# Context attention with 16 heads: GpSimd's softmax product of a unit as one operation or as two, first tile ahead

## The reference

```python
q = (query @ Wq + bq).reshape(B, Nq, H, D).transpose(0, 2, 1, 3)
k = (key_value @ Wk + bk).reshape(B, Nkv, H, D).transpose(0, 2, 1, 3)
v = (key_value @ Wv + bv).reshape(B, Nkv, H, D).transpose(0, 2, 1, 3)
attn = jnp.einsum('bhqd,bhkd->bhqk', q, k) * scale
attn = jnp.clip(attn, -CLAMP, CLAMP)
attn = jax.nn.softmax(attn, axis=-1)
x = jnp.einsum('bhqk,bhkd->bqhd', attn, v).reshape(B, Nq, Cq)
return x @ Wo + bo
```

## Time and profile before

| | |
|---|---|
| median of 3 runs | 3066.73 us |
| the profiled execution | 3068.3 us |
| its span on the core | 3066.6 us |
| mean granted clock of PE, of full speed | 0.92 |
| PE busy (matmul) | 2623.7 us, 86% |
| PE's weight loads busy | 1882.0 us, 61% |
| DVE busy | 1443.6 us, 47% |
| ACT busy | 1294.5 us, 42% |
| POOL busy | 891.2 us, 29% |
| POOL, L1438, all three context attentions | 436.0 us, 192 operations |

### The profile page before, as it was taken

How to read it: one execution, slowest core, us unless ns; L and a number is a source line. 1 busy time by engine, 2 the same in 40 slices (tenths; PEclk the granted TensorE clock), 3 DMA queues, 4 the chain that set the end, 5 groups by cost and what they waited for, 6 DMA issues and landing times. The chain is left out here.

```text
span 3066.6 us, 55571 instructions
## 1 busy us (share of the span) xinstructions
PE 2623.7 (86%) x18272; PEld 1882.0 (61%) x18273; DVE 1443.6 (47%) x3490; ACT 1294.5 (42%) x3858; POOL 891.2 (29%) x572
## 2 busy tenths in 40 slices
PE   5746999979787989999599877899959997988899
PEld 2335666656455556666489734566649996876554
DVE  5695888931534234444522376666650003553200
ACT  1334677832443123333233222677733332772222
POOL 3264455510001022222133243455522222330000
PEclk8867999979898999999799987999979998998999
DMA  2000000000241010000367600000045554004100
GB/s 105 1 0 28 17 20 20 16 30 0 58 105 52 0 45 21 15 15 15 126 207 237 204 33 33 22 15 20 15 181 171 177 184 134 1 17 113 56 12 13
DMA packets 108488, 194.38 MB, mean 63 GB/s; under 512 B 56532, under 2 KB 81060, under 8 KB 96596
## 3 DMA queue, kind: packets, MB, share of 16 engines
q1 hardware_dynamic: 93986, 166.80, 16.9%
q0 software_dynamic: 6816, 18.62, 2.1%
q10 hardware_dynamic: 7570, 7.47, 0.8%
HBM read 174.16 MB, written 18.71 MB: 63 GB/s over the span
## 5 line engine op out<-in xcount | busy, mean ns | idle before, releaser
L1438 POOL TENSOR_TENSOR L_xattn_p<-L_xattn_p,L_xattn_ri 112x1500 f32<-112x1500 f32 (+1 forms) x192 | 436.0, 2271 | 566.2 <-DVE L_xattn_ri L1746 566.2
L1651 ACT ACTIVATE L_xattn_pT<-ps 125x448 f32<-125x448 f32 (+1 forms) x576 | 256.5, 479 | 358.4 <-PE ps L1542 357.8
L1542 PEld LDWEIGHTS ps<-ident,L_xattn_p 112*125 112x125 f32 x1920 | 255.8, 191 | 121.2 <-ACT L_xattn_pT L1651 41.7
L1542 PE MATMUL ps<-ident,L_xattn_p 112*125 112x112 f32 x1920 | 292.0, 284 | 41.8 <-POOL L_xattn_p L1438 29.1
L1663 ACT ACTIVATE L_xattn_p<-L_xattn_sa,L_xattn_ng 112x375 f32<-112x375 f32 x512 | 304.8, 601 | 16.4 <-DVE L_xattn_ng L1762 10.7
L1093 PEld LDWEIGHTS ps<-L_ffn_xsT,L_ffn_w 128*128 128x128 f32 x2240 | 265.4, 195 | 7.0 <-issue 1.9
L1093 PE MATMUL ps<-L_ffn_xsT,L_ffn_w 128*128 128x128 f32 x2240 | 266.5, 278 | 2.4 <-ACT L_ffn_xsT L1123 2.4
L276 POOL TENSOR_TENSOR ln_rstd<-ln_tmp,half 112x8 f32<-112x8 f32 x26 | 44.4, 1722 | 703.7 <-DVE ln_tmp L225 526.5
L1155 DVE TENSOR_TENSOR L_ffn_y<-ps,L_ffn_pack 128x256 f32<-128x256 f32 x70 | 29.7, 425 | 365.4 <-PE ps L1102 365.4
L1102 PE MATMUL ps<-L_ffn_weights,L_ffn_hT 128*128 x840 | 192.9, 379 | 2.3 <-DVE L_ffn_hT L1167 2.3
L1564 PE MATMUL ps<-L_xattn_kT,L_xattn_qm 32*112 32x375 f32 (+1 forms) x1280 | 173.3, 524 | 11.2 <-DVE L_xattn_ng L1759 5.8
(11 more groups left out here) (415 smaller groups left out, 5113.2 us busy)
## 6 DMA issues: line engine op xcount, KB each, us to landing
L_ffn_w<-in_L_ffn_experts SPq DMA_DIRECT2D x74, 1024.0 KB
L_xattn_src<-in_ctx SPq DMA_DIRECT2D x48, 375.0 KB, 3.0
L_attn_toeplitz<-L_attn_h SPq DMA_DIRECT2D x4, 3136.0 KB, 24.0
L_ffn_weights<-in_L_ffn_experts SPq DMA_DIRECT2D x8, 1028.0 KB, 17.2
L_xattn_keys<-in_ctx SPq DMA_DIRECT2D x16, 281.2 KB, 6.0
L_xattn_rows<-in_ctx_rows SPq DMA_DIRECT2D x16, 281.2 KB
L_ffn_weights<-in_L_ffn_experts SPq DMA_DIRECT2D x8, 516.0 KB, 8.7
L_ffn_w<-in_L_ffn_experts SPq DMA_DIRECT2D x4, 1026.0 KB, 9.5
```

The lines of the kernel that those rows point to most:

```text
L1438: g.tensor_tensor(P[:, m % 4, :, :], P[:, m % 4, :, :], ri[:, m % 4, :].unsqueeze(2).broadcast_to([T, W, S2]), ALU.mult).then_inc(s["prob_ ...
L1542: last = pe.transpose(turned(t)[:, j * T:(j + 1) * T], P[:, m % 4, j, kc * KW:(kc + 1) * KW], k.ident[0:T, 0:T])
L1651: act.activation(PT[:, m % 4, kc, :, :].rearrange("p h t -> p (h t)"), turned(t), ACT.Copy).then_inc(s["pt_ev_a"].sem, 1)
```

## The change

In the stages with `copied` true POOL's product of a unit is issued as two operations, the first on columns 0 to 124 of each head, the second on columns 125 to 374. Each raises `prob_done` by one. PE waits for the first before tile 0 and for the second before tile 1. With `copied` false there is one share of all columns, as before.

```diff
+    shares = (slice(0, KW), slice(KW, S2)) if copied else (slice(0, S2),)
...
                     g.wait_ge(*s["ri_done"].at(i * U + m + 1))
-                    g.tensor_tensor(P[:, m % 4, :, :], P[:, m % 4, :, :],
-                                    ri[:, m % 4, :].unsqueeze(2).broadcast_to([T, W, S2]),
-                                    ALU.mult).then_inc(s["prob_done"].sem, 1)
+                    for at in shares:
+                        g.tensor_tensor(P[:, m % 4, :, at], P[:, m % 4, :, at],
+                                        ri[:, m % 4, :].unsqueeze(2).broadcast_to([T, W, at.stop - at.start]),
+                                        ALU.mult).then_inc(s["prob_done"].sem, 1)
...
                     t = m * KN + kc
-                    if kc == 0:
-                        pe.wait_ge(*s["prob_done"].at(i * U + m + 1))
+                    if kc < len(shares):
+                        pe.wait_ge(*s["prob_done"].at((i * U + m) * len(shares) + kc + 1))
                     pe.wait_ge(*s["pt_ev_a"].at(i * U * KN + t - 1))
...
-              prob_done=units, pt_mm=units * KN, pt_ev_a=units * KN, pv_mm=units // PVS, ot_ev=B,
+              prob_done=units * len(shares), pt_mm=units * KN, pt_ev_a=units * KN, pv_mm=units // PVS, ot_ev=B,
```

## The result

The changed kernel takes 3058.17 us, the median of 11 runs (3056.24 to 3062.59), against 3066.73 us for the kernel before (11 runs, 3062.49 to 3071.94). The ratio is 0.9974, 95% interval 0.9965 to 0.9983: 8.6 us faster, more than the 6.1 us that were called the smallest change to be told. The profiled execution took 3060.1 us.

What follows compares the result with a forecast made beforehand. PE was taken as the bound, losing nearly only its wait for POOL. Gains of 4.1 us (first attention), 5.0 (second) and 0.5 (tail) made 9.6 us, so a median of 3057.1 us, range 3051 to 3064.

Steps and rivals of the forecast that it cites:

- GpSimd's price: POOL's product at L1438: 186 ns fixed and 1.668 ns an element, so 1.02 and 1.85 us, the pair 2.83.
- Rival (d): POOL's two operations at 2.1 ns an element: pair 3.48 us, kernel slower by 11.7 us, 3078.4; chance 8%.
- 0.43 us taken from behind the wait, 0.14 given back: Tile 0's four PE transposes leave the wait, POOL's pair ends later: 0.29 gained a unit, taken as 0.28 us.
- The 0.5 us for the tail: First attention's end: last wait precedes twelve half-pace transposes, so tile 0 is worth about 1.0 us, 0.5 more.
- the sum had 14.5 places: First attention: 29 waits, two a batch, one of them on the loop: 14.5 x 0.28 = 4.1 us.
- Rival (a): DVE's order sets the first attention's pace; only second attention and tail gain: 5.5 us, 3061.2; chance 15%.
- The added wait at nothing: PE's one more semaphore wait a unit, 128 times, costs nothing; bounded by 0.05 us each, 6 us in all.
- The wait ahead of tile 1: In the profile after, PE's wait for POOL moves ahead of tile 1, about 0.75 us in the second attention.
- The second attention's 5.0 us: 18 PE waits for POOL in the second attention, each shortened by 0.28 us: 5.0 us.
- both signs of this: Forecast wrong if batches move under 0.15 us with the pair as priced, or another PE wait grows by POOL's loss.
- Rival (b): Mask row takes the port between POOL's operations, the second starting 0.35 us or more late: 3062; chance 4%.
- allowed for with 1 to 2 us: PE's clock may fall differently in later stages; 1 to 2 us allowed for it in the range.

Runs made afterwards that it cites:

- run 3: Kernel before, with PE waiting for the same single product once more ahead of tile 1; 3066.79 us, ratio 1.0002.
- run 6: Changed kernel with the cut behind the second tile (POOL's first operation 4 x 250 elements, second 4 x 125), mask row not moved; 3045.80 us, ratio 0.9930.
- run 5: The change in the second attention (layer 2) alone, the first as in the kernel before; 3067.37 us, ratio 0.9999.
- run 1: Changed kernel with DVE's mask row in the second attention moved to the start of its step, when GpSimd is idle; 3051.95 us, ratio 0.9954.
- run 4: The change in the first attention (layer 0) alone, the second as in the kernel before; 3060.59 us, ratio 0.9980.
- run 7: Changed kernel with the cut behind the second tile and the mask row moved to the start of its step; 3044.74 us, ratio 0.9927.
- run 8: Changed kernel with three POOL operations, one for each tile, and the mask row moved; 3035.18 us, ratio 0.9890.
- run 2: Kernel before with only the mask row moved to the start of its step; 3067.34 us, ratio 1.0001.

## Why the prediction was right, and where it was not

The number was right (3057.1 against 3058.17, inside 3051 to 3064). Its parts:

- *GpSimd's price* held to 3 ns on both operations, and the pair took 2.84 us (2.83 forecast). Rival (d), the dearer element, is out. L1893's row of 112 elements was the right witness.
- *0.43 us taken from behind the wait, 0.14 given back*: the first attention's batches fell by 0.28 or 0.29 us. Its stage gave 4.5 us where 4.6 were forecast. The 0.5 us for the tail are not in it: the long stretch between projections at the stage's end, 14.91 us, became 14.57, hardly more than any batch gave. 0.28 us in each of 16 batches makes the 4.5 by itself; the sum had 14.5 places. Rival (a), DVE's order as the bound there, is out.
- *The added wait at nothing*: shown by run 3.
- *The wait ahead of tile 1* was forecast at 0.75 us in the second attention and was 0.56: tile 0's four transposes, standing alone, keep PE busy for 0.69 us and not for 0.43. The gain behind the wait is still 0.43, the eight transposes' 1.12 less 0.69.
- *A reading*: DVE is not quite busy without a break from 502.70 to 508.91; it has two gaps of 0.15 us, ahead of its operations at 506.70 and 507.28. For neither does the trace name another engine.
- *The second attention's 5.0 us* is the step that failed. The words were: "DVE is idle enough in that stage (13.5 us of 20) to take this up before it next holds PE." The mask row did end 0.15 us later, as written, but what DVE does next is the four maxima that hold PE's next scores, with no idle time between. Over a batch DVE had 6.5 us to spare; between POOL's end and PE's next scores it had 0.26 us at most, since in the kernel before DVE's last maximum ended at 2055.51 and the scores started, with no wait, at 2055.77. The split needed 0.28 of it from the one side, and the mask row 0.15 from the other. In the changed kernel the scores start 0.06 us after the last maximum ends (2050.83, 2050.89), so 0.20 of the 0.26 could be used: 0.20 less 0.15 leaves 0.05 us, and a batch got 0.06 shorter, 0.7 us in twelve batches. The prediction had named both signs of this: a batch that moves by less than 0.15 us with the pair as priced, and a wait of PE on DVE's maxima that grows. By them the forecast was wrong for the second attention. The share of idle time was used for a question that only the timeline answers.
- *Rival (b)*, the port passing to DVE between the two operations, has a mechanism that occurs, as I read run 6. It did not happen in the change, for the reason given (0.45 us too late), and where it happens it costs GpSimd's second operation 0.11 us and not the 0.35 that was feared, while DVE gets its row done in 0.59 us in place of 1.43.
- *The total* came out right in part by luck. The first attention gave 4.5 us and the second 0.5 to 1.1 (run 5); the measured 8.6 has some 3 us more. In the three kernels with the first attention split as in the change (the change, runs 1 and 4), a stretch at the start of the expert stage behind it, from PE's L578 to its L425, took 15.8 or 15.9 us, in the four with the old one 18.6. The granted clock there is the third number from the right, of before and of after:

```profile
659.99:678.62 18.63, 17.07 (x48) 11.45 (x49) 5.54 (x8) 2.40 (x5) 0.00 (x0) 0.50 0.00 0
```

```profile
655.90:671.76 15.86, 14.28 (x49) 9.18 (x49) 5.53 (x8) 2.40 (x5) 0.00 (x0) 0.61 0.00 0
```

Half of full speed (1.2 GHz) throughout in the one, 0.61 on the mean in the other, in the same stretch of the program, which began 4.1 us earlier. An earlier start is not enough for it: in run 6 the stretch began at 649.19 us, 6.7 us earlier still, and took 18.6 us again, and so it did in runs 7 and 8. Over the program's last 210 us the three kernels took 1.6 to 2.2 us more (211.1 to 211.6 against 209.4 or 209.5). So the clock's levels fall differently from kernel to kernel, and some us come or go with that. It was allowed for with 1 to 2 us. With 4.5, 0.5 to 1.1, 2.8 and -2 the account stands near 6 us; what makes the rest of the 8.6 is open, and the interval of the total is 2.8 us either way. The two halves run by themselves (runs 4 and 5) gave 5.5 us and nothing to be told.

## To carry to other kernels

When two engines' paths into a third lie close, price the slack at that place, from its own rows in the timeline, before the first path is shortened: a share of idle time over a batch says nothing of it. Where a long operation feeds a consumer piece by piece, cut it where the consumer cuts it, and check what each piece leaves waiting; here the cut behind the first tile took 0.28 us off a batch of the first attention and 0.06 off one of the second, the cut behind the second tile 0.7 and 0.83, and three pieces, with the mask row moved, 0.7 and 1.09. An operation of DVE that GpSimd holds off is worth moving to where GpSimd is idle, but only once it is on the path; before that the move gave nothing.

## What the runs showed of the hardware

- GpSimd's product with a spread-out factor costs 186 ns and 1.668 ns an element in rows of 125 and 250 with gaps as in rows of 375 without, to 3 ns; two of them in a row take 0.04 us less than their sum.
- DVE's mask row (375 elements, SBUF to SBUF, from bytes) takes 0.355 us with GpSimd idle, and otherwise ends 0.2 us after the GpSimd operation that was running when it was issued: 1.43 us beside the one operation, 1.58 beside the two of the change, 0.59 where the first of two ended 0.38 us after its issue. GpSimd's next operation then lost 0.11 us. The Trainium skill, page "SBUF — State Buffer", section "SBUF: two separate sides", calls this an exclusive lock, and the trace agrees, with DVE held off by GpSimd (1.43 us for 0.355) and GpSimd by DVE (0.11 us).
- The clock of PE at the entrance of the second attention differs from profile to profile. Here are the first 40 us of the stage, in the kernel before and in run 4, where this stage is the same:

```profile
1916.53:1956.53 40.00, 33.01 (x260) 20.31 (x264) 26.90 (x99) 23.93 (x69) 15.30 (x6) 1.00 0.07 20
```

```profile
1905.75:1945.75 40.00, 35.08 (x228) 21.45 (x232) 23.26 (x88) 20.16 (x58) 11.99 (x5) 0.85 0.07 20
```

The four kernels whose second attention is that of before, mask row apart (before, runs 2, 3 and 4), took 340.0, 346.0, 343.3 and 343.4 us for it, though their batches are alike to 0.01 us. In the profiled execution of the change it even took 342.9. A change of 1 us in such a stage is to be read from its steady batches, or from stages with the same clock at their entrance, not from the total.
